# Reordering the stages of a phase on TensorE: convolution stages in one stretch, transposition and linear layer in another

## The chip, the cores and the metric

The kernel runs on one core of one Trainium2 chip. The metric is the time of one execution in microseconds on the device. The engines of the core are TensorE (PE; its weight loads are shown as PEld), VectorE (DVE), ScalarE (ACT), GpSimd (POOL) and SyncE (SP), which issues the DMAs. Each has its own queue and works through it in order; semaphores order the engines against one another.

## The reference

Input x holds 128 samples of 32 channels by 512 positions. Four layers follow one another. Each applies to x a chain of modulated one-dimensional convolutions (32 to 32 channels, 3 taps, weights scaled per sample by a style vector), and then a linear map over the 512 positions, with a residual:

```python
TYPES = ('same', 'upsample', 'same', 'downsample')
for i, typ in enumerate(TYPES):                       # convolutions of a layer
    out = _layer(out, style, weights[i], biases[i], mod_w[i], mod_b[i], typ)
# then, with y = out, a linear map of layer l over the last axis, added to x:
#   l = 0: y @ W.T + bias + low-rank updates (the same for all samples)
#   l = 1: y @ W_base.T + b + mixture of 8 low-rank adapters, top 2 by a router
#   l = 2: y @ kernel + bias + low-rank update per sample block (gate) + shared one
#   l = 3: y @ W_up.T + 4 low-rank experts, the best one by gate_w + expert_bias
```

All of it is in float32.

## The kernel before, in words

**Data.** 128 samples are 8 groups of 16. A group is a tile of 128 partitions (4 blocks of 32 channels) by 4 rows by 512 positions. A *phase* n is one layer of one group; groups go in pairs, so `PHASES` is 32, `STEP` is 8 phases for the four layers of a pair, `layer(n)` is `n % 8 // 2`. The residual stream of a group stays in SBUF in `x[g]`.

**Set-up.** A first program (about 68 us) makes the tables of scales and the effective weights. The main program follows.

**Convolution part of phase n** (small tiles, several at once on the array, fp32):
- `conv0(n)` (L1009, matmuls at L1003): first convolution, reads `xs` (x scaled, by POOL, L716). 96 matmul instructions, tiles of 32 by 32.
- `products(n)` (L1017, matmuls at L1027): products of the weights of two convolutions, from `w2s` (POOL, L685); ACT copies them out (`raw_v`, `wv`; L760, L762), POOL sums them to the blurred weights `wv` (`blurred`, L698, three instructions). 160 short matmuls.
- `conv2(n, 0)` and `conv2(n, 1)` (L1033, matmuls at L1052): upsampling, blur and third convolution in one, even and odd positions; 112 matmuls each. Evacuated to `y2` by ACT (L747) and DVE (L861), then DVE corrects the two ends (L868, semaphore `y2_ends`).
- `down(n, 0)` and `down(n, 1)` (L1058, matmuls at L1068): last convolution, 48 matmuls each, evacuated to `y3` (ACT L753, DVE L875).

**Linear part of phase m** (full array):
- `turn(m)` (L1073): 16 transpositions; ACT makes the high part `y3t_hi` (L768), DVE the low part `y3t_lo` (L881). The two parts are float32r, and a product is made of three passes (`PASSES`: hi by hi, hi by lo, lo by hi).
- `base(m, b)` (L1133, matmuls at L1137), four blocks b of 12 matmuls, then on DVE `residual(m, b)` (L895).
- In layers 1 and 3 `adapter` (L1081), `to_tokens` (L1111), a routing chain `gated` on DVE (L909), `adapter_turn` (L1123) and `adapted` (L1142).
- In two phases of eight (`EFF`: `m % 8` is 1 or 4, both in layers without adapters) `effective` (L1099): four matmuls, added by DVE to `w_raw` giving `w_sum` (L957), the weights of layer 2 of a later phase.

**Banks.** The eight PSUM banks are two sets of four, `bank_a` and `bank_b`, with fixed parts: `bank_b` takes `conv0`, `conv2(·,0)`, the adapters, `base` and `effective`; `bank_a` takes `products`, `conv2(·,1)`, `down` and `turn`.

**Order before.** PE's queue is written out by hand (L1178 to L1212). Iteration n, with m = n - 1: `conv0(n)`, `turn(m)`, `conv2(n,0)`, `conv2(n,1)`, the adapter and first block or blocks of the linear layer of m, `products(n+1)`, the rest of the linear layer, `down(n,0)`, `down(n,1)`. So the linear layer of the phase before lies inside the convolutions of this one. The loops of the other engines (POOL L706, ACT L808, DVE L969, SP L635) follow this order. `effective` goes in halves into the banks that blocks 0 and 1 have used, and PE waits for DVE's addition before block 2.

Of the kernel before, what the change touches and what calls it, by code (L numbers as in the profile page):

```python
# [9 lines left out]
P = 128  # L10
# [42 lines left out]
PAD = 2  # L53
# [431 lines left out]
def main_program(nc, ctx, io, keep, scratch):  # L485
# [38 lines left out]
    z_ps, logit_ps = bank_b[0], bank_b[1]  # L524
    zt_ps = logit_ps

    lin_ps = [bank_b[2], bank_b[3], bank_b[0], bank_b[1]]
# [75 lines left out]
    with nc.Block() as block:  # L603
# [74 lines left out]
        def _(pool):  # L678
# [26 lines left out]
            blurred(0)  # L705
            for n in range(PHASES):  # L706
# [11 lines left out]
                if n - 1 in MADE_IN:  # L718
                    u = MADE_IN[n - 1]
                    raw = w_sum if u % USES in (2, 3) else w_raw  # L720
                    for k in range(KB):
                        pool.wait_ge(w_hi, made(u, k + 1))
                        nc.gpsimd.tensor_tensor(w[u % 2][1][:, k], raw[:, k], w[u % 2][0][:, k].bitcast(F32),
                                                ALU.subtract).then_inc(w_lo, 1)
                if l < LAYERS - 1:
# [4 lines left out]
                if n + 1 < PHASES:  # L730
                    scaled_weights(n + 1)
                    blurred(n + 1)

        @block.scalar
        def _(act):
            a = nc.scalar

            def evacuate_0(n):
                act.wait_ge(c0_done, n + 1)
                for r in ON_ACT:  # L740
                    a.activation(y0[:, r, PAD:PAD + LEN], bank_b[r][:], ACT.Identity, bias=column(n, T_B, r), scale=column(n, T_A, r)).then_inc(y0_act, 1)  # L741

            def evacuate_2(n, u):
                scale, bank = (T_A + 2, T_A2)[u], (bank_b, bank_a)[u]
# [4 lines left out]
            def evacuate_3(n):  # L749
                for u in range(2):  # L750
                    act.wait_ge(dn_done, 2 * n + u + 1)
                    r = ON_ACT[u]
                    a.activation(y3[:, r], bank_a[r][:], ACT.Identity, bias=keep["cb3"][:, layer(n):layer(n) + 1], scale=column(n, T_A + 3, r)).then_inc(y3_act, 1)  # L753

            def products(n):
# [3 lines left out]
                for r in range(ROWS):  # L759
                    a.activation(raw_v[:, r, 1:RAW + 1].rearrange("p k o -> p (k o)"), bank_a[r][:, 0:RAW * CH],  # L760
                                 ACT.Copy).then_inc(raw_ready, 1)
                    a.activation(wv[:, r, TAPS_V:].rearrange("p k o -> p (k o)"),  # L762
                                 bank_a[r][:, RAW * CH:(RAW + GHOSTS) * CH], ACT.Copy).then_inc(ghosts_ready, 1)

            def turned(m):
                for k in range(KB):
                    act.wait_ge(tr_done, tiles(m, k + 1))
                    a.activation(y3t[0][:, k], bank_a[k][:], ACT.Copy).then_inc(y3t_hi, 1)  # L768

            def adapter(m):  # L770
# [3 lines left out]
                if l == 1:  # L774
                    a.activation(z_raw[:], z_ps[:], ACT.Copy)
                    a.activation(logits[:], logit_ps[0:E1], ACT.Copy).then_inc(z_raw_ready, 1)
                elif l == 3:
                    a.activation(z_raw[0:Z23], z_ps[0:Z23], ACT.Copy).then_inc(z_raw_ready, 1)
# [6 lines left out]
            def adapter_turned(m):  # L785
                if layer(m) in (1, 3):
                    rows = E1 * R1 if layer(m) == 1 else len(PASSES) * E3 * R3
                    act.wait_ge(zt_done, before(m, (1, 3)) + 1)
                    a.activation(zt[0][0:rows], zt_ps[0:rows], ACT.Copy).then_inc(zt_hi, 1)
# [18 lines left out]
            for n in range(PHASES + 1):  # L808
                m, convolve, linear = n - 1, n < PHASES, n > 0
                if convolve:  # L810
# [3 lines left out]
                if convolve:  # L814
                    evacuate_2(n, 0)
                    evacuate_2(n, 1)
                if linear:
                    adapter(m)
                    exponentials(m)
                if n + 1 < PHASES:  # L820
                    products(n + 1)
                if linear:
# [3 lines left out]
                if convolve:  # L826
                    evacuate_3(n)

        @block.vector
        def _(dve):  # L830
# [20 lines left out]
            def evacuate_0(n):  # L851
                dve.wait_ge(c0_done, n + 1)
                for r in ON_DVE:
                    v.tensor_scalar(y0[:, r, PAD:PAD + LEN], bank_b[r][:], column(n, T_A, r), column(n, T_B, r),  # L854
                                    ALU.mult, ALU.add).then_inc(y0_dve, 1)

            def evacuate_2(n, u):
                scale, bank = (T_A + 2, T_A2)[u], (bank_b, bank_a)[u]
# [12 lines left out]
            def evacuate_3(n):  # L871
                for u in range(2):
                    dve.wait_ge(dn_done, 2 * n + u + 1)
                    r = ON_DVE[u]
                    v.tensor_scalar(y3[:, r], bank_a[r][:], column(n, T_A + 3, r), keep["cb3"][:, layer(n):layer(n) + 1],  # L875
                                    ALU.mult, ALU.add).then_inc(y3_dve, 1)

            def turned(m):
                for k in range(KB):
                    dve.wait_ge(y3t_hi, tiles(m, k + 1))  # L880
                    v.tensor_tensor(y3t[1][:, k], bank_a[k][:], y3t[0][:, k].bitcast(F32),  # L881
                                    ALU.subtract).then_inc(y3t_ready, 1)

            def residual(m, b):
# [10 lines left out]
                v.tensor_tensor(result, lin_ps[b][:], x[g][:, b], ALU.add).then_inc(x_ready, 1)  # L895
# [13 lines left out]
            def gated(m):  # L909
# [6 lines left out]
                if l == 1:  # L916
                    then(v.tensor_copy(lg[:], logit_ps[:, 0:ROWS * E1].rearrange("p (t e) -> p t e", e=E1)))
                else:
                    then(v.tensor_tensor(lg[:, :, 0:e], z_ps[:].rearrange("p (t c) -> p t c", c=P)
# [413 lines left out]
```

## Time and profile before

| | us |
|---|---|
| median of 3 runs | 1300.11 |
| lowest, highest | 1298.98, 1308.33 |
| profiled execution, its time | 1306.01 |
| its span, first to last instruction | 1304.2 |
| mean granted clock of TensorE | 0.987 |

| engine | busy us | share of the span |
|---|---|---|
| PE (matmuls) | 1233.0 | 95% |
| PEld (weight loads) | 704.6 | 54% |
| POOL | 546.2 | 42% |
| DVE | 496.3 | 38% |
| ACT | 356.1 | 27% |

The span comes from one profiled execution; the runs without a profile give the median. A row of the timeline gives the start, the duration of the row (from the first start to the last end, where it holds several instructions), engine, line, operation, output and inputs, number of instructions, and in brackets the idle time ahead of it with what ended it. Ends of matmuls are modelled, so that the distance between two starts says more than a duration. The granted clock is that which the chip let TensorE have, 1.00 being 2.4 GHz and 0.50 being 1.2 GHz.

### The profile page before, as it was taken

How to read it: one execution, taken by the hardware profiler on the slowest of the kernel's cores; microseconds unless marked ns; L12 is line 12 of the kernel's file. 1: busy time of each engine (PE TensorE's matmuls, PEld its weight loads, DVE VectorE, ACT ScalarE, POOL GpSimd, SP SyncE). 2: the span in 40 equal slices, each digit the busy share in tenths (PEclk: the TensorE clock that was granted, in tenths of full speed). 3: DMA queues.
4: the chain of work that ended last, by engine and by line, in shares of the span. 5: the costliest groups of instructions: out<-in, count | busy, mean ns of one | idle time of the engine just before them, and what ended most of it. 6: DMA issues, size and time to landing. Idle time of an engine off the chain costs nothing.

```text
span 1304.2 us, 45847 instructions
## 1 busy us (share of the span) xinstructions
PE 1233.0 (95%) x21400; PEld 704.6 (54%) x21400; DVE 496.3 (38%) x975; ACT 356.1 (27%) x757; POOL 546.2 (42%) x417
## 2 busy tenths in 40 slices
PE   5847999999999999999999999999999999999997
PEld 5323556555555555565565555565565554665555
DVE  5612324344333333434333333434333434433343
ACT  2213313223322222313223222312323222312321
POOL 3156641444443442644323543644413544634400
PEclk9968999999999999999999999999999999999999
DMA  8232300002221200000301300000211200000101
GB/s 285 114 105 101 115 17 2 2 3 59 98 105 62 99 3 2 3 2 25 134 27 42 131 3 2 2 2 13 103 53 58 99 3 2 2 2 3 67 2 65
DMA packets 20828, 65.66 MB, mean 50 GB/s; under 512 B 4032, under 2 KB 4416, under 8 KB 16160
## 3 DMA queue, kind: packets, MB, share of 16 engines
q1 hardware_dynamic: 18960, 60.85, 12.8%
q8 instruction: 168, 2.75, 0.9%
q10 hardware_dynamic: 1680, 1.89, 0.5%
q14 instruction: 20, 0.16, 0.0%
HBM read 43.85 MB, written 18.87 MB: 48 GB/s over the span
## 4 chain that ended last, share of the span: by engine, by line
PE 87%; DVE 4%; POOL 1%; issue 1%; ACT 0%; DMA 0%; DVEq 0%; POOLq 0%
PE bank_b L1137 26%; PE bank_a L1068 13%; PE bank_a L1052 11%; PE bank_b L1052 11%; PE bank_b L1003 8%; PE bank_b L1095 5%; PE bank_a L1078 5%; PE bank_a L1027 3%; PE bank_b L1149 2%; PE bank_b L1118 1%; DVE w_sum L957 1%; PE bank_b L1130 1%; POOL xs L716 1%; POOL sum_v L698 1%; DVE z L939 1%
## 5 line engine op out<-in xcount | busy, mean ns | idle before, releaser
L698 POOL TENSOR_TENSOR sum_v<-raw_v 128x768 f32<-128x768 f32 x32 | 58.9, 1842 | 626.5 <-ACT raw_v L760 626.5
L1137 PE MATMUL bank_b<-w_hi,y3t_hi 128*128 128x512 f32 x512 | 210.0, 410 | 12.4 <-DVE w_sum L957 12.1
L1137 PE MATMUL bank_b<-w_hi,y3t_lo 128*128 128x512 f32 x512 | 203.0, 396 | 2.2 <-issue 2.2
L1137 PE MATMUL bank_b<-w_lo,y3t_hi 128*128 128x512 f32 x512 | 202.4, 395 | 0.1
L1068 PE MATMUL bank_a<-y,w_down 64*32 64x512 f32 x3072 | 173.6, 594 | 1.5 <-ACT wv L762 1.5
L1052 PE MATMUL bank_a<-y,wv 32*64 32x512 f32 (+2 forms) x3584 | 145.8, 480 | 2.3 <-issue 2.3
L1052 PE MATMUL bank_b<-y,wv 32*64 32x512 f32 (+2 forms) x3584 | 142.3, 480 | 1.8 <-ACT y L741 1.8
L895 DVE TENSOR_TENSOR x<-bank_b,x 128x512 f32<-128x512 f32 x96 | 66.4, 692 | 202.2 <-PE bank_b L1137 166.0
L753 ACT ACTIVATE y<-bank_a,cb,tab 128x512 f32<-128x512 f32 x64 | 49.7, 776 | 319.4 <-PE bank_a L1068 319.4
L1003 PE MATMUL bank_b<-xs,cw 32*32 32x512 f32 x3072 | 112.0, 615 | 15.3 <-POOL xs L716 15.3
L1137 PEld LDWEIGHTS bank_b<-w_hi,y3t_hi 128*128 128x128 f32 x512 | 96.8, 189 | 50.9 <-DVE w_sum L957 15.6
L1137 PEld LDWEIGHTS bank_b<-w_hi,y3t_lo 128*128 128x128 f32 x512 | 96.6, 189 | 25.9 <-issue 3.1
L1068 PEld LDWEIGHTS bank_a<-y,w_down 64*32 64x32 f32 x3072 | 55.3, 106 | 102.2 <-issue 102.2
L1137 PEld LDWEIGHTS bank_b<-w_lo,y3t_hi 128*128 128x128 f32 x512 | 97.0, 189 | 20.3 <-issue 0.6
L716 POOL TENSOR_TENSOR xs<-x,tab 128x512 f32<-128x512 f32 x96 | 97.3, 1043 | 8.9 <-DVE x L895 8.9
L1052 PEld LDWEIGHTS bank_a<-y,wv 32*32 32x32 f32 (+1 forms) x3584 | 45.0, 114 | 100.9 <-issue 100.4
L875 DVE TENSOR_SCALAR y<-bank_a,tab,cb 128x512 f32<-128x512 f32 x64 | 51.8, 810 | 121.4 <-PE bank_a L1068 121.4
L1003 PEld LDWEIGHTS bank_b<-xs,cw 32*32 32x32 f32 x3072 | 48.0, 104 | 76.5 <-issue 48.1
L854 DVE TENSOR_SCALAR y<-bank_b,tab 128x512 f32<-128x512 f32 x64 | 48.9, 807 | 100.8 <-PE bank_b L1003 100.8
L1052 PEld LDWEIGHTS bank_b<-y,wv 32*32 32x32 f32 (+1 forms) x3584 | 44.7, 114 | 76.4 <-issue 73.3
L881 DVE TENSOR_TENSOR y3t_lo<-bank_a,y3t_hi 128x512 fp32r<-128x512 f32 x128 | 79.5, 684 | 15.0 <-ACT y3t_hi L768 15.0
L861 DVE TENSOR_SCALAR y<-bank_a,tab 128x512 f32<-128x512 f32 x64 | 48.9, 806 | 90.4 <-PE bank_a L1052 90.4
(172 smaller groups left out, 1553.0 us busy)
## 6 DMA issues: line engine op xcount, KB each, us to landing
w_hi<-w_scratch SPq DMA_DIRECT2D x9, 1024.0 KB, 5.8
w_lo<-w_scratch SPq DMA_DIRECT2D x9, 1024.0 KB, 8.0
x_in<-in_x SPq DMA_DIRECT2D x32, 256.0 KB, 4.1
out_x<-out_tile SPq DMA_DIRECT2D x32, 256.0 KB, 2.4
w_raw<-w_scratch SPq DMA_DIRECT2D x3, 1024.0 KB, 9.8
w_scratch<-w_hi SPq DMA_DIRECT2D x3, 1024.0 KB, 3.9
w_scratch<-w_lo SPq DMA_DIRECT2D x3, 1024.0 KB, 6.9
w<-in_w SPq DMA_DIRECT2D x2, 1024.0 KB, 13.5
```

The lines of the kernel that those rows point to most:

```text
L698: ins = g_.tensor_tensor(dst[:, :, at:at + count].rearrange("p r k o -> p r (k o)"), src[:, :, 0:count].rearrange("p r k o -> p r (k o)"), ...
L716: nc.gpsimd.tensor_tensor(xs[:, b, 1:LEN + 1], src[:, b], column(n, T_S, b).broadcast_to((P, LEN)), ALU.mult).then_inc(xs_ready, 1)
L753: a.activation(y3[:, r], bank_a[r][:], ACT.Identity, bias=keep["cb3"][:, layer(n):layer(n) + 1], scale=column(n, T_A + 3, r)).then_inc(y3_ ...
L875: v.tensor_scalar(y3[:, r], bank_a[r][:], column(n, T_A + 3, r), keep["cb3"][:, layer(n):layer(n) + 1], ALU.mult, ALU.add).then_inc(y3_dve, 1)
L881: v.tensor_tensor(y3t[1][:, k], bank_a[k][:], y3t[0][:, k].bitcast(F32), ALU.subtract).then_inc(y3t_ready, 1)
L895: v.tensor_tensor(result, lin_ps[b][:], x[g][:, b], ALU.add).then_inc(x_ready, 1)
L1003: ins = pe.matmul(banks[r][CH * c:CH * (c + 1)], weights[rows, l, block_], src[rows, (r + c) % ROWS, 1 + shift:1 + shift + LEN], start=(i ...
L1052: ins = pe.matmul(banks[r][to:to + CH * count, at:at + length], wv[rows, a, tap:tap + count].rearrange("p t o -> p (t o)"), y0[rows, a, st ...
L1068: ins = pe.matmul(bank_a[2 * u + h][CH * a:CH * (a + 1)], keep["down"][rows, layer(n), t], y2[u][rows, c, t:t + LEN], start=(t == 0), stop ...
L1078: ins = pe.transpose(bank_a[k][:, P * b:P * (b + 1)], y3[:, b, P * k:P * (k + 1)], ident[:])
L1095: ins = pe.matmul(ps[0:rows], a_l[ai][:, k, col:col + rows], y3t[yi][:, k], start=(k == 0 and i == 0), stop=(k == KB - 1 and i == 2))
L1137: ins = pe.matmul(lin_ps[b][:], y3t[yi][:, k, P * b:P * (b + 1)], w[use(m) % 2][wi][:, k], start=(k == 0 and i == 0), stop=(k == KB - 1 an ...
```

## The change

The order of an iteration n (m = n - 1) becomes: `conv2(m,0)`, `conv2(m,1)`, `products(n)`, `down(m,0)`, `down(m,1)`, `conv0(n)`, then `turn(m)` and the whole linear layer of m. The bank sets take turns: in phase m `banks_p(m)` takes `conv2(m,0)`, `products(m+1)`, `conv0(m+1)` and then `base(m)`, and `banks_q(m)` takes `conv2(m,1)`, `down(m)`, `turn(m)`, the adapters and `effective(m)`. The first block of the linear layer is split into its high passes (which wait for each quarter of `y3t_hi`) and its low passes. `effective` is done in one piece behind block 0. On POOL `blurred(n)` moves from the end of iteration n - 1 into iteration n, behind `xs(n)` and the low parts of the weights, and ahead of the additions of the output bias (`xb_ready`); `scaled_weights(1)` goes ahead of the loop. ACT's and DVE's queues follow. What is computed stays the same, and so does the number of instructions of each kind; SP's part of the code is not touched.

```diff
-    z_ps, logit_ps = bank_b[0], bank_b[1]
-    zt_ps = logit_ps
-    lin_ps = [bank_b[2], bank_b[3], bank_b[0], bank_b[1]]
+    def banks_p(m):
+        return (bank_a, bank_b)[m % 2]
+    def banks_q(m):
+        return (bank_b, bank_a)[m % 2]
+    # z_bank, logit_bank, zt_bank: banks_q(m)[0], [1], [2]
...
             scaled_weights(0)
             blurred(0)
+            scaled_weights(1)
             for n in range(PHASES):
...
+                if n:
+                    blurred(n)
                 if l < LAYERS - 1:
...
-                if n + 1 < PHASES:
+                if 1 <= n and n + 1 < PHASES:
                     scaled_weights(n + 1)
-                    blurred(n + 1)
...
             def conv0(n):
-                if n >= 2:
-                    pe.wait_ge(x_ready, tiles(n - 2, ROWS))
-                    if (n - 2) % STEP in EFF:
-                        pe.wait_ge(w_sum_ready, summed(n - 2) + KB)
                 pe.wait_ge(xs_ready, tiles(n, ROWS))
+                pe.wait_ge(raw_ready, tiles(n, ROWS))
+                pe.wait_ge(ghosts_ready, tiles(n, ROWS))
...
             def products(n):
                 if n:
-                    pe.wait_ge(y2_ends, 2 * n)
+                    pe.wait_ge(y2_ends, 2 * n - 1)
...
             def conv2(n, u):          # u == 0
+                    if n:
+                        pe.wait_ge(y3t_ready, tiles(n - 1, KB))
+                        if (n - 1) % STEP in EFF:
+                            pe.wait_ge(w_sum_ready, summed(n - 1) + KB)
                 elif n:
-                    pe.wait_ge(y3t_ready, tiles(n - 1, KB))
-                banks = (bank_b, bank_a)[u]
+                    pe.wait_ge(x_ready, tiles(n - 1, ROWS))
+                banks = (banks_p(n), banks_q(n))[u]
...
             def down(n, u):
                 pe.wait_ge(y2_ends, 2 * n + 2)
-                if n + 1 < PHASES:
-                    pe.wait_ge(raw_ready, tiles(n + 1, ROWS))
-                    pe.wait_ge(ghosts_ready, tiles(n + 1, ROWS))
...
+            def base_hi(m, b):
+                for k in range(KB):
+                    if b == 0:
+                        pe.wait_ge(y3t_hi, tiles(m, k + 1))
+                    for wi in range(2):
+                        pe.matmul(banks_p(m)[b][:], y3t[0][:, k, P * b:P * (b + 1)], w[use(m) % 2][wi][:, k],
+                                  start=(k == 0 and wi == 0), stop=False)
+            def base_lo(m, b):        # the four lo passes; b == 0 waits for y3t_ready of each k
...
+            def weights(m):
+                if m + 1 < PHASES:
+                    pe.wait_ge(y0_act, evacuated(m + 1))
+                    pe.wait_ge(y0_dve, evacuated(m + 1))
...
+            def linear_plain(m):
+                weights(m)
+                base(m, 0)
+                effective(m)
+                for b in range(1, ROWS):
+                    base(m, b)
+            def linear_adapted(m):
+                weights(m)
+                base_hi(m, 0)
+                adapter(m)            # its hi passes first, then its lo passes
+                base_lo(m, 0)
+                to_tokens(m)
+                base(m, 1)
+                base(m, 2)
+                adapter_turn(m)
+                base(m, 3)
+                pe.wait_ge(zt_ready, before(m, (1, 3)) + 1)
+                for b in range(ROWS):
+                    adapted(m, b)
...
             for n in range(PHASES + 1):
                 m, convolve, linear = n - 1, n < PHASES, n > 0
+                if linear:
+                    conv2(m, 0)
+                    conv2(m, 1)
+                if linear and convolve:
+                    products(n)
+                if linear:
+                    down(m, 0)
+                    down(m, 1)
                 if convolve:
                     conv0(n)
                 if linear:
                     turn(m)
-                # ... conv2(n), adapter, blocks, products(n + 1), blocks, down(n)
+                    linear_adapted(m) if layer(m) in (1, 3) else linear_plain(m)
```

## Rows read from the trace of the kernel before

**Rows 1.** The page: PE's busy time, and the chain by engine.

```profile
PE 1233.0 (95%) x21400; PEld 704.6 (54%) x21400; DVE 496.3 (38%) x975; ACT 356.1 (27%) x757; POOL 546.2 (42%) x417
...
PE 87%; DVE 4%; POOL 1%; issue 1%; ACT 0%; DMA 0%; DVEq 0%; POOLq 0%
```

**Rows 2.** Timeline of PE: five starts of `down` (start us, us, then the instructions).

```profile
534.10 5.38 PE L1068 MATMUL bank_a<-y,w_down 64*32 64x512 f32 x96
...
577.38 5.38 PE L1068 MATMUL bank_a<-y,w_down 64*32 64x512 f32 x96
...
612.74 5.39 PE L1068 MATMUL bank_a<-y,w_down 64*32 64x512 f32 x96
...
645.39 5.38 PE L1068 MATMUL bank_a<-y,w_down 64*32 64x512 f32 x96
...
682.48 5.38 PE L1068 MATMUL bank_a<-y,w_down 64*32 64x512 f32 x96
```

**Rows 3.** Timeline of PE: the iteration from 612.74 to 645.39.

```profile
618.05 3.40 PE L1003 MATMUL bank_b<-xs,cw 32*32 32x512 f32 x96
621.39 1.97 PE L1078 MATMUL bank_a<-ident,y 128*128 128x128 f32 x16
623.29 4.45 PE L1052 MATMUL bank_b<-y,wv 32*64 32x512 f32 x112
627.67 4.45 PE L1052 MATMUL bank_a<-y,wv 32*64 32x512 f32 x112
632.04 0.50 PE L1137 MATMUL bank_b<-w_hi,y3t_hi 128*128 128x512 f32 x1
632.38 0.40 PE L1137 MATMUL bank_b<-w_lo,y3t_hi 128*128 128x512 f32 x1
...
634.71 0.40 PE L1137 MATMUL bank_b<-w_hi,y3t_lo 128*128 128x512 f32 x1
635.04 1.85 PE L1027 MATMUL bank_a<-w2s,w_up 32*32 32x96 f32 x160
636.82 0.51 PE L1137 MATMUL bank_b<-w_hi,y3t_hi 128*128 128x512 f32 x1
```

**Rows 4.** Timelines of ACT and DVE in the same iteration.

```profile
622.84 2.06 ACT L768 ACTIVATE y3t_hi<-bank_a 128x512 fp32r<-128x512 f32 x4
...
623.47 2.48 DVE L881 TENSOR_TENSOR y3t_lo<-bank_a,y3t_hi 128x512 fp32r<-128x512 f32 x4 [0.44 <-ACT y3t_hi L768]
...
632.25 1.53 DVE L861 TENSOR_SCALAR y<-bank_a,tab 128x512 f32<-128x512 f32 x2 [2.65 <-PE bank_a L1052]
633.81 0.17 DVE L868 TENSOR_TENSOR y<-y,tab 128x8 f32<-128x8 f32 x1
```

**Rows 5.** Waits (total us, times, longest); timeline of the copies in layer 1.

```profile
PE bank_b L1137 <- DVE w_sum L957: 12.1, 8, 1.5
...
559.07 0.40 PE L1137 MATMUL bank_b<-w_hi,y3t_hi 128*128 128x512 f32 x1
...
559.76 0.57 ACT L776 ACTIVATE logits<-bank_b 8x512 f32<-8x512 f32 x1
```

**Rows 6.** Timeline of PE: the start of the main program.

```profile
83.96 5.16 PE L1003 MATMUL bank_b<-xs,cw 32*32 32x512 f32 x96 [11.76 <-POOL xs L716]
...
101.74 2.48 PE L1027 MATMUL bank_a<-w2s,w_up 32*32 32x96 f32 x160 [2.03 <-DVE y L868]
105.76 6.76 PE L1068 MATMUL bank_a<-y,w_down 64*32 64x512 f32 x96 [1.54 <-ACT wv L762]
116.07 4.68 PE L1003 MATMUL bank_b<-xs,cw 32*32 32x512 f32 x96 [3.54 <-POOL xs L716]
...
146.84 5.38 PE L1068 MATMUL bank_a<-y,w_down 64*32 64x512 f32 x96
```

**Rows 7.** Timeline of PE inside `products`; then busy times, granted clock by window.

```profile
172.93 0.94 PE L1027 MATMUL bank_a<-w2s,w_up 32*32 32x96 f32 x67 [1.63 <-issue]
...
174.00:176.00 2.00, 2.00 (x5) 1.61 (x6) 0.00 (x0) 1.27 (x8) 0.77 (x1) 0.50 0.03 8
```

## What bounds the kernel, what the change does to it, and the forecast

> **What bounds the kernel now.** I read the page's first part and its chain, then the timeline of TensorE (PE) over whole iterations, then ScalarE (ACT) and VectorE (DVE) in the same stretch, then the waits and the start. PE is busy in 95% of the span and carries 87% of the chain [rows 1]; apart from its own weight loads no other engine passes 42%. So only three things can move the time: what PE issues (unchanged in kind and number by this edit), the gaps at the edges between stages, and the waits.
>
> An iteration runs from the start of one `down` stage to the next. Its length is 43.28 us where the linear layer is that of layer 1 (534.10 to 577.38), 35.36 us in layers 0 and 2 with the weight update `effective` (577.38 to 612.74), 32.65 us without it (612.74 to 645.39), and 37.09 us in layer 3 (645.39 to 682.48) [rows 2]. From the `down` that starts at 146.84 [rows 6] thirty iterations follow (linear phases m = 1 to 30: 7 plain, 8 with update, 8 of layer 1, 7 of layer 3). Besides these there is the start, up to 146.84, and the tail.
>
> **The change part by part, PE first.**
>
> *Edges.* A full-array matmul follows another after 0.23 us (632.38 stands behind a first one that took 0.34) [rows 3]. So a full-array stretch behind small tiles costs 0.11 us at its first matmul. A small stage behind a full-array one starts 0.33 us after the last matmul instead of 0.23 (634.71 to 635.04) [rows 3], 0.10 us. `products` alone has both edges, inside the linear layer; after the change it stands between `conv2` and `down`, and the full-array work is one stretch. `turn` to the linear layer loses its edges too. Per iteration about 0.3 us of edges goes. The Trainium skill, "TensorEngine Tiling (Array Packing)", section Key Properties, says that a change of tiling mode drains TensorE; the rows agree that it costs something. The sum goes by the rows, and its full worth is a rival below.
>
> *The wait before `down` (new).* `down(m)` needs both evacuations of `conv2(m,1)` and the end correction. Before, a block of the linear layer and `products` lay between. Now only `products(n)` does, 1.78 us (635.04 to 636.82) [rows 3]. In the rows `conv2(·,1)` ends at E = 632.04 (start of the next stage), DVE evacuates from 632.25 for 1.53 us and the correction starts at 633.81 for 0.17 us [rows 4], so it ends at E + 1.94. To PE's start I add 0.11, between 0.05 and 0.15 (in the start-up, where nothing covers this chain, PE stood 2.03 us on it [rows 6]). `down` starts at E + 2.05, whatever `products` gains by following without a change of tile shape. Shown as idle time this is 0.2 us if `products` runs as before, up to 0.8 if it starts during the end of `conv2`. Behind this wait stand `down`, `conv0`, `turn` and all the rest of PE's queue.
>
> *The wait before the linear layer (new).* Call C the start of `turn`, 621.39. ACT first evacuates `conv0`, then starts `y3t_hi` at 622.84 = C + 1.45; four take 2.06 us, so the ends lie at C + 2.05, 2.54, 3.02, 3.51. DVE's `y3t_lo` start at 623.47 and take 2.48 us for four: ends C + 2.8 to C + 4.56 [rows 4]. Before, 8.75 us of `conv2` hid all of it. Now the first block wants `hi` at C + 2.10: two matmuls per quarter, 0.23 each plus about 0.1 where the weight load is exposed; the eight end at C + 4.06. The four `lo` matmuls follow without a further wait; the block ends at C + 4.99. Before, `turn` and first block took 1.90 + 3.00 = 4.90 us. The split into hi and lo passes is what makes the new wait cheap: waiting for all of `lo` would give C + 4.61 + 2.79 = C + 7.4.
>
> *Plain iteration.* down 5.31, conv0 3.34, turn and block 0 4.99, three blocks of 12 matmuls 8.37, edge 0.09, two `conv2` 8.75, to the next `down` 2.05: 32.90 against 32.65, +0.25 us. The evacuations of `down`'s second half (under 1 us) hide under `conv0` (3.34); the raw copies on ACT (1.4 us) under `down`.
>
> *With update.* Before, PE waits for `w_sum` 12.1 us in 8 waits [rows 5], since the blocks share the banks of the update. The four products of the update (0.93) now go to the banks that `turn` has left, and DVE's additions have three blocks (8.4 us) before `conv2` wants the banks. 32.90 + 0.93 = 33.83 against 35.36: -1.53 us.
>
> *Layer 1.* ACT copies `z_raw` and then `logits`; the latter starts at 559.76 and takes 0.57, so it ends 1.26 us after PE's next matmul starts (559.07) [rows 5]. The cover was a whole block (2.79), now four matmuls (0.93): about +0.38. The gating chain on DVE had block 1 and `products`, now blocks 1 and 2 (5.6 us), and gives back 0.1. Together +0.5 us. *Layer 3*: one short copy, hidden; 37.51 against 37.09, +0.4 us.
>
> *Other queues.* POOL now runs `blurred(n)` (about 6.3 us) behind `xs(n)` and the low parts of the weights; it waits for the raw copies, some 12 us into the iteration, ends at about 18 and is wanted at over 32. `xb` (5 us) and `w2s` behind it end at about 24; `w2s` is wanted 8.75 us into the next iteration. SP waits for `xb` before its loads of x, and these are wanted an iteration later. In layer 3 the last two residuals wait for output tiles to be stored; they end about 3.9 us after PE leaves the linear layer, and `conv2(·,1)` wants them at 4.4: nothing, with little room.
>
> *Start.* Before, POOL makes `wv(1)` ahead of `xs(1)`, so that `conv0(1)` starts at 116.07 with a wait of 3.54, and `products(1)` stands 2.03 us for the evacuations; then `down` runs 6.76 instead of 5.38 us at the lower clock [rows 6]. After: `w2s(1)` goes ahead of `xs(0)` (+0.83), so `conv0(0)` starts at 84.8 (was 83.96 [rows 6]), `conv2` at 91.7 (behind its evacuation), which ends at 100.5, `down(0)` 102.55, `conv0(1)` 107.9, `turn(0)` 111.2, the linear layer ends at 124.6, two `conv2` to 133.4, `down(1)` at 135.5. `xs(1)` needs the x tile, which is reloaded after `xb(0)` (89.7): ready by about 99. That is 11.3 us ahead of 146.84. Not all of it is sure: two stalls of PE on nothing the profile names lie in that stretch before and may come again. I take 10 us; bounds 0 and 11.3.
>
> *Tail.* Layer 3's four last matmuls stand at the end, so the residuals start later; the wait for all of `lo` goes. I make this +0.5 us.
>
> **Sum.** 7 x 0.25 + 8 x 0.51 + 7 x 0.42 - 8 x 1.53 = -3.5 us over thirty iterations. 1304.2 - 10 - 3.5 + 0.5 = 1291.2 us of span; with the 1.8 us around it 1293.0 against the profiled 1306.01. The median of before is 1300.11, 0.45% less than that run: 1287 us.
>
> **The rivals.**
>
> *The clock falls (slower).* At 174 to 176 us the granted clock is 0.50 (1.2 of 2.4 GHz), behind a stall of 1.63 us inside `products`; in these 2 us PE ran five full-array matmuls, where 0.23 us apart gives nearly nine; over the 3 us that it lasted I put the loss at 1.4 us [rows 7]. `down` at that clock lost 1.38 us [rows 6]. Against it: eight waits of 1.5 us for `w_sum` [rows 5] fell at full clock. The place is `products` plus the wait before `down`, 2 to 2.6 us of thin work in each of 30 iterations; it decides if the idle time reaches about 1.5 us. Then 30 x 1.4 = 42 us: 1329. The Trainium skill, "TensorE: Matmul & The Clock Gate", sections HAM oscillation and Part 4, warns of idle gaps and says that transposes don't count as busy. The second place would be `turn` plus its wait, 2.1 us. Chance 0.09.
>
> *Fetch stalls (slower).* PE shows eight waits on "issue" alone, the longest 1.63 [rows 7], all before 490 us, two of them in `products`. With `conv2` (224 matmuls) and `products` (160) now back to back, PE's queue is drained faster. One of 1 us per iteration gives 1287 + 30 = 1317. Part of each would vanish in the wait before `down`. Chance 0.08.
>
> *The start gives nothing* (x reload, or the same stalls and clock): 1287 + 10 = 1297. Chance 0.15.
>
> *The waits are longer*: if each quarter of the first block exposes its weight load and the output tiles bind, +0.4 us x 30: 1299. Chance 0.10.
>
> *The drains pay in full* (the rule of the tiling page as mechanism): the wait at the linear layer vanishes in what the edges give, -0.3 us x 30: 1278. It can't help at `down`, where the chain of evacuations sets the start. Chance 0.08.
>
> **Numbers.** My forecast holds with 0.50, by itself 1280 to 1295. The range of all but the two slow rivals is 1272 to 1304. 1% is 13 us, about what a measurement of this kernel can tell from no change; the forecast lies on that edge. Faster by over 1%: somewhat over half of the forecast's 0.50 and the drains, 0.36; slower 0.17; between them 0.47.
>
> **What would show it.** The waits for `w_sum` by L1137 gone. A wait of `down` for the correction on DVE, about 30 times, 0.2 to 0.8 us. A wait of the first block for `y3t_hi`. From `down` to `down` 32.9, 33.8, 43.8 and 37.5 us. `down(1)` at about 136. It is wrong if the granted clock in the regular part is below 1.00, if "issue" waits come in each iteration, or if `conv2(·,1)` waits for residuals.

## The result and the profile after

| | before | after |
|---|---|---|
| median, us | 1303.06 (4 runs) | 1343.41 (4 runs) |
| lowest, highest, us | 1298.98, 1308.33 | 1336.84, 1349.27 |
| profiled execution: time, span, us | 1306.01, 1304.2 | 1349.27, 1347.5 |
| mean granted clock in it | 0.987 | 0.976 |

The ratio is 1.0306, interval 1.0241 to 1.0371: slower by 3%, where no change or a gain of 1% was forecast. The time lies 39 us above the upper end of the range.

The page of the kernel after, its first part (busy time, share, instructions), the chain by engine, and the queue that brings the instructions (packets, MB, share):

```profile
PE 1249.6 (93%) x21400; PEld 719.4 (53%) x21400; DVE 503.4 (37%) x975; ACT 358.4 (27%) x757; POOL 547.2 (41%) x417
...
PE 82%; ACT 5%; issue 3%; DVE 3%; POOL 1%; DMA 0%; DVEq 0%
...
q8 instruction: 168, 2.75, 0.8%
```

PE issues the same 21400 matmuls, but "issue" stands at 3% of the chain where it was 1% [rows 1], and PE itself is busy 16.6 us longer. The waits of PE after (engine, tile, line, what it waited for: us in total, times, longest); the set-up and the first phase have been left out except for `xs`:

```profile
PE bank_a L1032 <- issue: 13.6, 8, 4.1
PE bank_b L1010 <- POOL xs L728: 12.5, 1, 12.5
...
PE bank_b L1032 <- issue: 10.7, 7, 2.4
...
PE bank_b L1074 <- issue: 9.9, 3, 4.5
...
PE bank_a L1074 <- issue: 3.6, 3, 2.9
PE bank_a L1146 <- ACT y3t_hi L781: 3.5, 16, 0.2
PE bank_a L1074 <- DVE y L879: 3.4, 8, 1.9
PE bank_b L1146 <- ACT y3t_hi L781: 3.3, 15, 0.2
```

The waits for `w_sum` [rows 5] are gone, and the new waits for `y3t_hi` are 0.2 us each, as forecast. What is new beyond that is "issue" in `products` (L1032) and in the `down` behind it (L1074). Over all lines "issue" holds 38.4 us in 23 waits, twelve of them of 1.85 us or more; before it was 7.4 us in eight, none as long as that.

Timeline of PE after, one iteration near the end and the stages at the start of the next:

```profile
1237.95 0.64 PE L1032 MATMUL bank_b<-w2s,w_up 32*32 32x96 f32 x23
1238.74 1.57 PE L1032 MATMUL bank_b<-w2s,w_up 32*32 32x96 f32 x128 [0.15 <-issue]
1242.21 0.27 PE L1032 MATMUL bank_b<-w2s,w_up 32*32 32x32 f32 x9 [1.90 <-issue]
1242.41 7.08 PE L1074 MATMUL bank_a<-y,w_down 64*32 64x512 f32 x96
1249.41 3.40 PE L1010 MATMUL bank_b<-xs,cw 32*32 32x512 f32 x96
...
1274.90 1.87 PE L1032 MATMUL bank_a<-w2s,w_up 32*32 32x96 f32 x148
1278.86 0.28 PE L1032 MATMUL bank_a<-w2s,w_up 32*32 32x32 f32 x12 [2.09 <-issue]
1279.07 5.38 PE L1074 MATMUL bank_b<-y,w_down 64*32 64x512 f32 x96
```

In both iterations PE issues 151 and 148 of the 160 matmuls of `products`, stands for 1.90 and 2.09 us with nothing that it waits for, and then issues the last ones. In the first of them two things are lost: the stall, and 1.70 us because `down` then takes 7.08 instead of 5.38 us [rows 2]. Windows over that place (us, busy time of PE, PEld, DVE, ACT, POOL with instructions, granted clock, DMA share, GB/s):

```profile
1240.00:1242.00 2.00, 0.31 (x26) 0.21 (x24) 0.08 (x1) 0.00 (x0) 0.00 (x0) 1.00 0.00 0
1242.00:1244.00 2.00, 1.79 (x33) 0.75 (x40) 0.00 (x0) 1.36 (x8) 0.14 (x1) 0.77 0.03 8
1244.00:1246.00 2.00, 2.00 (x24) 0.53 (x16) 0.00 (x0) 0.00 (x0) 1.92 (x2) 0.50 0.00 0
1246.00:1248.00 2.00, 2.00 (x42) 0.73 (x34) 0.81 (x1) 0.78 (x1) 1.92 (x2) 0.88 0.00 0
```

The clock is 1.00 while PE stands and 0.50 (1.2 GHz) just after. The DMA share is 0.00 during the stall: nothing competes for the DMA engines then.

**Where the 56.3 us are.** The forecast span was 1291.2, the measured one 1347.5. Up to `down(1)`, forecast at 136.8 and begun at 142.31, 5.5 us; from there to the last `down`, 50.6 us; the tail 0.3. The 50.6 I take apart with the timeline. Waits on "issue" from 142 us on are 34.8 us against 6.4 before, which the forecast had carried over: 28.4. The stages of `down`, without waits inside, take 25.0 us more than 31 times 5.31, against 1.2 before (that 1.2 lies in the last one, in both): 23.8. Of these, eight stages that ran partly at the lower clock make 16.4 (five of them 1.70 each, as the one shown, three 2.3 to 2.9), and eleven at full clock that are 0.3 to 1.0 us longer make 7.4. Together 52.2, where 50.6 are to be explained; the difference is waits for DVE that vanish where PE comes late anyway. Every other stage has its length: `conv0` 3.34, `turn` with its wait 2.19, the two `conv2` 8.56 in the median.

### The profile page after: what moved, and what is told of

It is laid out like the page before. It is cut to its first block, busy times and chain, and to the rows that moved or that the text cites. A ratio compares the mean times of both kernels' runs of the same rounds, so it can differ in the third digit from the quotient of the medians.

```text
span 1347.5 us, 45826 instructions
## 1 busy us (share of the span) xinstructions
PE 1249.6 (93%) x21400; PEld 719.4 (53%) x21400; DVE 503.4 (37%) x975; ACT 358.4 (27%) x757; POOL 547.2 (41%) x417
## 3 DMA queue, kind: packets, MB, share of 16 engines
HBM read 43.85 MB, written 18.87 MB: 47 GB/s over the span
## 4 chain that ended last, share of the span: by engine, by line
PE 82%; ACT 5%; issue 3%; DVE 3%; POOL 1%; DMA 0%; DVEq 0%
PE bank_a L1061 11%; PE bank_b L1061 11%; PE bank_a L1146 9%; PE bank_b L1146 9%; PE bank_b L1074 7%; PE bank_a L1074 7%; PE bank_b L1010 4%; PE bank_b L1154 4%; PE bank_a L1154 4%; PE bank_a L1010 4%; ACT y L754 3%; DVE y L872 2%; PE bank_b L1099 2%; PE bank_a L1099 2%; PE bank_b L1032 1%
## 5 line engine op out<-in xcount | busy, mean ns | idle before, releaser
L1074 PE MATMUL bank_b<-y,w_down 64*32 64x512 f32 x1536 | 100.7, 646 | 11.6 <-issue 9.9
L1146 PE MATMUL bank_a<-w_hi,y3t_hi 128*128 128x512 f32 x256 | 103.7, 405 | 3.5 <-ACT y3t_hi L781 3.5
L1146 PE MATMUL bank_b<-w_hi,y3t_hi 128*128 128x512 f32 x256 | 103.8, 405 | 3.3 <-ACT y3t_hi L781 3.3
L1074 PE MATMUL bank_a<-y,w_down 64*32 64x512 f32 x1536 | 97.2, 630 | 7.1 <-issue 3.6
L1146 PE MATMUL bank_b<-w_lo,y3t_hi 128*128 128x512 f32 x256 | 101.1, 395 | 0.0
L1146 PE MATMUL bank_a<-w_lo,y3t_hi 128*128 128x512 f32 x256 | 101.1, 395 | 0.0
L743 POOL TENSOR_TENSOR x<-x,ob 128x512 f32<-128x512 f32 x64 | 80.0, 1289 | 0.0
L709 POOL TENSOR_TENSOR wv<-sum_v 128x1024 f32<-128x1024 f32 x32 | 75.9, 2371 | 2.5
L1154 PE MATMUL bank_b<-w_hi,y3t_lo 128*128 128x512 f32 x256 | 70.0, 395 | 0.0
L1154 PE MATMUL bank_a<-w_hi,y3t_lo 128*128 128x512 f32 x256 | 70.0, 395 | 0.0
```

Of the source, the lines that this page charges most:

```text
L709: ins = g_.tensor_tensor(dst[:, :, at:at + count].rearrange("p r k o -> p r (k o)"), src[:, :, 0:count].rearrange("p r k o -> p r (k o)"), ...
L743: nc.gpsimd.tensor_tensor(x[g][:, b], src[:, b], keep["ob"][:, l], ALU.add).then_inc(xb_ready, 1)
L1074: ins = pe.matmul(banks_q(n)[2 * u + h][CH * a:CH * (a + 1)], keep["down"][rows, layer(n), t], y2[u][rows, c, t:t + LEN], start=(t == 0), ...
L1146: pe.matmul(banks_p(m)[b][:], y3t[0][:, k, P * b:P * (b + 1)], w[use(m) % 2][wi][:, k], start=(k == 0 and wi == 0), stop=False)
L1154: ins = pe.matmul(banks_p(m)[b][:], y3t[1][:, k, P * b:P * (b + 1)], w[use(m) % 2][0][:, k], start=False, stop=(k == KB - 1 and l in (0, 2)))
```

## The experiments

Two theories stood at the start. One (theory F): instructions don't reach PE's queue fast enough for `products` when `conv2` runs right before it; the clock's falls and the longer `down` follow from these stalls. The other: the time is lost to the new order as such, in the edges between shapes (rival S) or in the idle time before `down` (rival I; 2.2 us of thin work in each iteration), whatever the queue has. Each ratio is to the kernel before, run again on the same chip. The four experiments without a ratio have one run each, so that a few us between two of them say nothing.

### Products issued twice, in the old order

```diff
 # kernel before, products(n)
-for s, at, first, count in (*((t, CH * t, 0, TAPS) for t in range(TAPS)), ...):
+for s, at, first, count in 2 * (*((t, CH * t, 0, TAPS) for t in range(TAPS)), ...):
```

> The kernel before, with the matmuls of products issued twice (the same values are written again). 160 more matmuls per phase in the middle of the linear layer, 1.78 us each phase. Theory F: 640 instructions in 3.6 us are more than the fetches give (256 per 3.3 us), so each phase waits another 2 to 4 us on issue: span 1304 + 57 + 64 to 128 = 1425 to 1490, waits on issue 64 to 128 us. Rivals S and I: the order of before is kept and nothing idles, so the span is 1304 + 57 = 1361 with under 15 us on issue.

Measured: 1481.27 us, span 1479.5, clock 0.949, against 1304.09 of before. Waits, timeline and the DMA view of one place (the last from 640 to 650 us in 40 slices of 0.25 us):

```profile
PE bank_a L1027 <- issue: 81.3, 45, 2.9
```

```profile
641.49 1.78 PE L1027 MATMUL bank_a<-w2s,w_up 32*32 32x96 f32 x152
645.31 1.96 PE L1027 MATMUL bank_a<-w2s,w_up 32*32 32x32 f32 x128 [2.03 <-issue]
649.33 0.68 PE L1027 MATMUL bank_a<-w2s,w_up 32*32 32x32 f32 x40 [2.06 <-issue]
```

```profile
GB/s 0 0 0 0 0 0 0 0 0 0 0 0 66 0 0 0 0 0 0 0 0 0 0 0 0 0 0 66 0 0 0 0 0 0 0 0 0 0 0 0
DMA packets 2, 0.03 MB, mean 3 GB/s; under 512 B 0, under 2 KB 0, under 8 KB 0
...
q8 instruction: 2, 0.03, 1.1%
...
q8 instruction: 208, 3.41, 0.9%
```

Between the two stalls PE issues 128 matmuls, with their weight loads 256 instructions. Two packets arrive in these 10 us, both in the queue of instructions; they start at about 643.1 and 646.9, and each stall ends 2.2 to 2.4 us after such a start. Over the whole run (last line) there are 208 packets where before has 168; 40 more for 5120 more matmuls and as many loads: one packet, 16 KB, for 256 instructions. In the records of all nine traces no two of them start closer than 3.25 us. `products` uses 320 instructions in 1.78 us [rows 3], so 256 of them in 1.4.

Besides the 57 us that the doubled matmuls take by themselves, 85.9 us of "issue" (all lines) came, where before has 7.4. The doubled part lies in the old place, between blocks of the linear layer, with no edge and no wait added. The stalls come from the burst itself: the theory of the queue holds, and one that needs the new place can't explain this run.

The Trainium skill, "Runtime: NRT & Kernel Launch", section Instruction fetch mechanics, says that instructions are brought in blocks of 16 KiB, 256 of them, and that this is mostly hidden because an engine dispatches more slowly than blocks arrive. The block size agrees with 256 instructions from stall to stall; that it is hidden doesn't, where PE uses a block in 1.4 us and none follows another in under 3.25.

### Shorter products, in the new order

```diff
 # kernel after, products(n), from phase 2 on: two of the five steps, 64 of 160 matmuls (phase 1: four steps)
-for s, at, first, count in (*((t, CH * t, 0, TAPS) for t in range(TAPS)), ...):
+for s, at, first, count in ((0, 0, 0, TAPS), (2, 2 * CH, 0, TAPS)):
```

> The changed kernel, with 64 instead of 160 matmuls in products from phase 2 on (the middle one of three taps and the edge terms are left out, so part of the computation is missing). Everything else stays, and down still starts when the evacuations of conv2 are done. Theory F: 192 instructions fewer per iteration behind conv2, so the waits on issue fall from 38 us to under 10, and the span to about 1305, although PE now idles 1.2 to 1.9 us before each down. Rival I: the idle time before down is longer than in the changed kernel, so the clock falls oftener and the span is at or above 1347.

Measured: 1289.18 us, span 1287.4, clock 0.990. Waits, and the timeline: a `down`, the `turn` behind it, and the four next starts of `turn` (layer 1, update, plain, layer 3 between them):

```profile
PE bank_a L1074 <- DVE y L879: 18.4, 16, 1.9
PE bank_b L1074 <- DVE y L879: 16.7, 16, 1.1
...
PE bank_b L1061 <- issue: 1.3, 1, 1.3
```

```profile
510.38 5.38 PE L1074 MATMUL bank_a<-y,w_down 64*32 64x512 f32 x96 [1.10 <-DVE y L879]
...
519.03 1.97 PE L1084 MATMUL bank_a<-ident,y 128*128 128x128 f32 x16
...
562.92 1.97 PE L1084 MATMUL bank_b<-ident,y 128*128 128x128 f32 x16
...
596.78 1.97 PE L1084 MATMUL bank_a<-ident,y 128*128 128x128 f32 x16
...
629.76 1.97 PE L1084 MATMUL bank_b<-ident,y 128*128 128x128 f32 x16
...
667.28 1.97 PE L1084 MATMUL bank_a<-ident,y 128*128 128x128 f32 x16
```

Less work in `products` can't shorten an iteration here, because `down` waits for the correction on DVE in its place: 1.10 us in 29 of 32 phases (35.1 in all), where the full `products` leave 0.2. So this run shows the new order with its waits and its edges as they are, and with a queue that is hardly ever short. "Issue" falls from 38.4 to 1.3 us. From 142 us on every `down` but one and the last takes 5.31 or 5.32 us, where after 19 of 31 take at least 0.28 us longer; the one takes 6.15, at full clock. The iterations are 43.89, 33.86, 32.98 and 37.52 us. That is the forecast of the prediction (43.8, 33.8, 32.9, 37.5), and the time with it; what I expected just before the run, about 1305, was 18 us too much. So the new order as such costs no more than the forecast had for it; the loss is the stalls and what follows on them.

The 29 idle stretches of 1.10 us before `down` brought no fall of the clock, so the thin work at that place isn't enough for one. The last `down`, which no `products` precedes, stands 1.92 us and then runs at the lower clock, 7.08 us.

### Products behind down

```diff
 # kernel after, order on PE; ACT's copies move along
     conv2(m, 1)
-    products(n)
     down(m, 0); down(m, 1)
+    products(n)
     conv0(n)
```

> The changed kernel with products between down and conv0. Nothing covers the evacuations before down, so PE idles about 2 us there in each of 31 iterations; products has left conv2. Theory F: waits on issue under 15 us; the idle time adds 1.8 us per iteration, about 55 us, to what the changed kernel would take without fetch waits (1291 to 1300): 1340 to 1355, a clock fall on a part of them. Rival I: 2 us of idle time lets the clock fall in most iterations, 1.7 us each: over 1390.

Measured: 1432.11 us, span 1430.3, clock 0.971: 77 us above the upper end expected, and in the range that rival I named (over 1390). The largest waits, and three stages of one iteration:

```profile
PE bank_b L1074 <- DVE y L879: 30.8, 16, 2.0
PE bank_a L1074 <- DVE y L879: 30.8, 16, 2.0
PE bank_a L1010 <- ACT wv L775: 24.7, 16, 1.6
PE bank_b L1010 <- ACT wv L775: 23.3, 15, 1.6
```

```profile
1147.94 7.08 PE L1074 MATMUL bank_a<-y,w_down 64*32 64x512 f32 x96 [1.92 <-DVE y L879]
1154.95 1.85 PE L1032 MATMUL bank_b<-w2s,w_up 32*32 32x96 f32 x160
1158.35 4.13 PE L1010 MATMUL bank_b<-xs,cw 32*32 32x512 f32 x96 [1.55 <-ACT wv L775]
```

Waits on "issue" fell to 7.9 us in six: behind `down`, which uses its 192 instructions in 5.31 us, `products` mostly finds the queue full. But `down` now stands 1.92 us in every iteration, and `conv0` 1.55 us more for ACT's copies of the products out of the banks that `conv0` writes. This second wait (48 us) I had overlooked: whatever is moved to the end of a stage takes its evacuation with it. So the run shows where the stalls go, and is no way to remove them. It also shows the other side of the clock: of the 31 `down` from 142 us on, each behind a wait of 1.92 to 1.98 us, ten ran at the lower clock at first and took 1.70 us longer, as the one shown (granted clock 0.56 from 1148 to 1151 us), with no "issue" wait ahead of them but one of 0.42 us. Idle time of this length lowers the clock sometimes, whatever PE waits for. Four `conv0` were slow in the same way (1.4 to 2.5 us longer, behind waits of 1.54 to 1.63 us, three of them with an "issue" wait inside the `products` ahead). Nine more `conv0` take 0.2 to 0.8 us longer at full clock, as the one shown (1.00 from 1158.4 to 1162.4 us): there the queue is short behind `products`, without a wait in the records. The falls are some 25 us in 14 iterations, not in most as rival I had it; without the 48 us of the second wait the span would lie under 1390.

### Conv0 between conv2 and down, products behind down

```diff
 # kernel after, order on PE; ACT, DVE and the waits follow
     conv2(m, 0); conv2(m, 1)
-    products(n)
+    conv0(n)
     down(m, 0); down(m, 1)
-    conv0(n)
+    products(n)
     turn(m)
```

> The changed kernel with another order of its small stages: conv2, conv2, conv0(n), down(m), products(n), turn(m), linear layer. The dense stage products no longer follows conv2; conv0 covers the evacuations that down waits for, and products covers those that turn waits for. Theory F (PE's instructions are fetched 256 at a time and never closer than 3.3 us apart, and products behind conv2 uses them faster): the waits of PE on issue fall from 38 us to under 10, the lower clock goes with them, and no wait of down for L879 is left; span 1278 to 1292. Rival S (small stages back to back cost by themselves, whatever their order): still over 1330. Rival I (the idle time before down lets the clock fall, and that is the loss): about as F here, so this run does not tell F and I apart.

Measured over three rounds: 1302.17 us (1299.69 to 1306.93) against 1304.09 (1300.49 to 1309.92), ratio 0.9987, interval 0.9969 to 1.0004. That is no difference, and 41 us less than the kernel after with the same instructions. Waits and one stall:

```profile
PE bank_a L1036 <- issue: 10.6, 7, 3.6
...
PE bank_b L1036 <- issue: 5.6, 6, 1.3
```

```profile
940.71 1.69 PE L1036 MATMUL bank_a<-w2s,w_up 32*32 32x96 f32 x140
...
943.73 0.31 PE L1036 MATMUL bank_a<-w2s,w_up 32*32 32x32 f32 x20 [1.34 <-issue]
```

The wait of `down` for DVE is gone, since `conv0` covers it. Stalls fell from 38.4 to 17.4 us (16 waits), not below 10 as expected. With the iterations of the run with shorter products and 0.3 us less in each of 30, the span would be 1278; the 16 us more of "issue" are most of what lies between that and 1300.2. The undisturbed iterations are 32.57, 33.5, 43.54 and 37.16 us, 0.3 shorter than those of the kernel after. So what runs ahead of `products` sets how often it stalls, but this burst can outrun the queue behind `down` too.

### Products in two parts, in the new order

```diff
 # kernel after, order on PE; ACT copies between its two evacuations of y3
     conv2(m, 1)
-    products(n)
+    products(n, 0)          # 64 matmuls
     down(m, 0)
+    products(n, 1)          # 96 matmuls
     down(m, 1)
```

> The changed kernel in its own order, nothing left out, with products cut in two: 64 matmuls behind conv2 as before, 96 between the halves of down. Theory F: the waits on issue fall from 38 us to under 10 and the clock stays up. The second part no longer hides in the wait for the evacuations, which costs 1.1 us and two changes of shape per iteration, 45 us in all against the run with short products (1287), so the span is 1320 to 1340. Rivals S and I (small stages back to back, or idle time before down, make the waits on issue): they stay near 38 us, and the span goes to 1365 or more.

Measured: 1339.29 us, span 1337.5, clock 0.985:

```profile
PE bank_a L1036 <- issue: 4.7, 3, 2.5
...
PE bank_b L1079 <- DVE y L881: 17.3, 16, 1.1
...
PE bank_a L1079 <- DVE y L881: 17.3, 16, 1.9
```

No matmul is left out and no edge taken away (two are added), and "issue" falls from 38.4 to 9.4 us: it is the burst's length that PE's queue can't follow. The time stays about where it was (at the upper end of what was expected), since the second part now lies in the open: `down(m, 0)` waits 1.10 us for DVE 28 times (34.6 in all), which the whole `products` had covered. Here, as in the run with shorter products, what fills the wait of `down` costs nothing, and what is taken out of it has to be paid elsewhere.

### Both: conv0 first, products in two parts

```diff
 # the kernel of "conv0 between conv2 and down", order on PE
     down(m, 0)
+    products(n, 0)          # 64 matmuls
     down(m, 1)
-    products(n)
+    products(n, 1)          # 96 matmuls
```

> The order of the spread kernel (conv2, conv2, conv0, down, products, turn), with products cut in two: its first 64 matmuls between the two halves of down, its last 96 behind down. No burst is longer than 192 instructions, under one fetch of 256. Theory F: waits on issue fall from 17 us to under 6; two more changes of tile shape cost 0.3 to 0.4 us per iteration (about 11 us), so the span is 1283 to 1296. If the waits on issue in the spread kernel have another cause than the burst, they stay at 15 us or more and the span is over 1305.

Measured over three rounds: 1299.84 us (1295.48 to 1304.05) against 1301.82 (1299.67 to 1308.51), ratio 0.9979, interval 0.9958 to 1.0000.

```profile
PE bank_a L1038 <- issue: 5.6, 5, 2.0
```

"Issue" is down to 8.6 us in eight waits, near the 7.4 of before, though not under 6 as expected. But the iterations are 32.88, 33.82, 43.85 and 37.48 us, again 0.3 longer than with `products` in one piece: two more edges between shapes, 0.15 us each. The gain in stalls (8.8 us) and the cost of the edges (30 times 0.3) cancel, and the two ratios, 0.9987 and 0.9979, can't be told apart. The span, 1296.1, lies just above the upper end expected.

### The update's banks alone, in the old order

The one term of the sum that gave a gain was that of the update. It doesn't need the new order: in the kernel before the matmuls of `effective` can also go to `bank_a`, which is free once the products have been copied.

```diff
 # kernel before, effective(m) on PE and DVE: all four products in one piece, behind block 1
-    for k in (2 * half, 2 * half + 1):
-        pe.matmul(bank_b[k][:], ...)
+    pe.wait_ge(raw_ready, tiles(m + 2, ROWS)); pe.wait_ge(ghosts_ready, tiles(m + 2, ROWS))
+    for k in range(KB):
+        pe.matmul(bank_a[k][:], ...)
 # linear layer
-    pe.wait_ge(w_sum_ready, summed(m) + 2)
 # down(n, 0)
+    pe.wait_ge(w_sum_ready, summed(n - 1) + KB)
```

> The kernel before with one part of the change alone: the four products of the update of the weights go, in one piece behind block 1, to the bank set that the linear layer doesn't use at that time (bank_a, free once the raw copies of products are out), so PE doesn't wait for w_sum. Order and banks of all else are those of before. Theory F: the 12.1 us of waits for w_sum are gone, the waits on issue stay at 7 to 10 us; span about 1292, ratio 0.990 to 0.993. If the gain of that part had been given back elsewhere (DVE late for the residuals, down waiting for w_sum), the span stays above 1300.

Measured over five rounds: 1292.79 us (1290.21 to 1298.93) against 1301.66 (1299.06 to 1309.78), ratio 0.9926, interval 0.9898 to 0.9953: faster by 0.7%, the best of all kernels here that compute everything. Its waits show none for `w_sum`, and "issue" at 7.6 us as before:

```profile
PE bank_b L1136 <- issue: 4.9, 5, 1.8
...
PE bank_a L1024 <- issue: 2.4, 2, 1.3
```

The waits for `w_sum` had been 12.1 us [rows 5], 0.9% of the time; 8.9 us came back.

## Why the prediction was wrong

**What held.** The lengths of the iterations: 32.9, 33.8, 43.8, 37.5 forecast, 32.98, 33.86, 43.89, 37.52 in the run with shorter products, and in the kernel after itself 37.50 where the queue isn't short (1279.07 to 1316.57). So the wait before `down` (0.21 us where it shows), the waits for `y3t_hi` (0.2), the end of the waits for `w_sum`, the price of layers 1 and 3 and the tail were right. That the plain iteration agrees within 0.1 us is in part luck, since three terms are off and cancel: two `conv2` take 8.57 us, not 8.75; from their end to `down` it is 2.18, not 2.05; `turn` and the linear layer take 13.59, not 13.45. The prediction took `products` behind `conv2` for no change of tile shape, but it is one, 32*64 to 32*32 [rows 3], and the full `products` take 1.97 us there instead of 1.78, which eats the cover of the wait. The start too: with no stall in it `down(1)` begins at 135.31 us in the run with shorter products, forecast 135.5 to 136 (the prediction counts two unnamed stalls up to 146.84 in the kernel before; the trace has one, 1.06 us at 137.60). The sum was right for a PE that always has its next instruction: 1291.2 us forecast, with the 7.4 us of "issue" of before in it, and 1287.4 measured there, with 1.3.

**The step that failed** is the one that costs the move of `products` at nothing but edges. I wrote that with `conv2` and `products` back to back "PE's queue is drained faster", priced it at one stall of 1 us per iteration (30 us) and gave it 0.08. It was the mechanism. Its size without what follows is 38.4 - 7.4 = 31 us, as that rival had it. That the size agrees is luck: there isn't one stall of 1 us per iteration but 23 in all, of 1.7 us on average. To this come 7.4 us in which `down` is starved at full clock without a wait in the records.

**The second rival came with it.** "The clock falls" was put down to the thin work of `products` and of the wait before `down` and given 0.09 as a case of its own. The shorter products, with 1.10 us of idle time at that place in 29 phases, show no fall there; the falls in the kernel after came where a stall of 1.85 us or more had gone before, in eight iterations, 16.4 us. So these weren't two rivals of which at most one comes: the second is what the first brings. Stalls, starved `down` stages and clock together, 31 + 7.4 + 16.4, are nearly all of the 56.3 us. With these three measured terms the forecast of the profiled run, 1293.0, becomes 1293 + 31 + 7 + 16 = 1347 us, against 1349.27. Of the signs that the prediction named for being wrong, two came: a granted clock below 1.00 in the regular part, and "issue" waits, though not in each iteration.

**What the rows had shown.** One could have seen it from the kernel before. Half of the reading was there: stalls on "issue" inside `products`, and a clock at 0.50 behind one of them [rows 7]. What was missing was a rate for each stage. 192 instructions of `down` take 5.31 us [rows 2], 192 of `conv0` 3.34, 448 of both `conv2` 8.75, 320 of `products` 1.78 [rows 3]; for 256 instructions that is 7.1, 4.5, 5.0 and 1.4 us, and in the linear layer, with one full-array matmul and its load every 0.23 us, about 30. Before, `products` stood between blocks of the linear layer, where the queue has all the time to fill; the change puts it behind 8.75 us of the stage that uses 256 in 5.0. The packets of instructions, 168 in the run, tell how many come at once.

**How a stall comes about.** All 23 stalls of the kernel after end 2.17 to 2.71 us after the start of a packet, and in 18 of them the packet before had started 4.2 us or more before that one (5.03 at the stall of 2.09 us). So it mostly isn't the least distance of 3.25 us that holds them up, but the time from asking for a packet to having it. Counting PE's records against the packets shows how far ahead the queue is filled (about 8 instructions per phase are not in the records, so the counts are good to some ten). In the slow linear layer a packet starts when some 250 to 300 instructions are still in hand, about one block. In the stalls of 1.85 to 2.16 us in or just behind `products` it starts 0.9 to 1.2 us after PE has begun its last block, with 45 to 91 instructions in hand, and these are used up in 0.4 to 0.65 us. From the start of the last block in hand to the end of the stall it is 3.4 to 3.7 us. So my estimate is that a block has to last some 3.5 us; in `conv2` it lasts 5.0, in `products` 1.4, and 3.5 less 1.4 is the size of these stalls. By this estimate, where in `conv2`, `products` or `down` a block happens to end decides whether an iteration has a stall, a longer `down` or neither.

**The longest stalls.** Those of 3.59, 2.91, 4.47 and 4.12 us (ending at 109.40, 147.15, 345.41 and 1042.36) are of another kind: their packet starts only 0.6 to 2.2 us after the stall has begun, at 107.20, 144.84, 343.18 and 1040.14, and just before that the kernel's own transfers are dense, 347 GB/s from 104 to 107 us, 342 from 142 to 144.8, 309 from 340 to 343 and 334 from 1036 to 1040 (columns as in the windows above):

```profile
1036.00:1040.00 4.00, 2.25 (x181) 1.78 (x149) 1.70 (x3) 1.45 (x2) 0.00 (x0) 1.00 0.85 334
```

In the 3 us ahead of the packets of the other stalls of 1 us and more it is 0 to 11 GB/s. That transfers delay the packets is likely by this, but no run moved them.

**What stays open.** Stalls in `products` come after 123 to 151 of its 160 matmuls; a kernel that moves one stage by a few instructions, to shift where the blocks end, wasn't run. Nor is it settled why a stall of 2.09 us at 1276.8 left the clock up and one of 1.90 at 1240.3 didn't; the rows only say that both happen.

## What to carry to other kernels

Count instructions per us, not only busy time, before packing short matmuls together: here a stage that used 256 instructions in 1.4 us went with 7.4 us of "issue" in the whole run between slow full-array matmuls, and with 38.4 us behind a stage that used 256 in 5.0 us. If a stall can be long enough to lower the clock, put both into one rival, with the slower stage behind it in its price. Where only one term of a reordering gives a gain, try that term alone: moving the update's four products to other banks gave 0.7%, and the whole new order lost 3%.

## What the runs showed of the hardware

- Packets of 256 PE instructions (16 KB) start at least 3.25 us apart in every trace here, even when the DMA engines carry nothing else. Between 1270 and 1290 us of the kernel after, with a stall of 2.09 us at 1276.8, the DMA view has four packets in all, in slices of 0.5 us:

```profile
GB/s 0 0 33 0 0 0 0 0 0 0 0 0 33 0 0 0 0 0 0 0 33 0 0 0 0 0 0 0 0 33 0 0 0 0 0 0 0 0 0 0
DMA packets 4, 0.07 MB, mean 3 GB/s; under 512 B 0, under 2 KB 0, under 8 KB 0
```

  The packet at about 1276.2 started 5.0 us after the one before it, and the stall ended 2.65 us after its start. Traffic of the kernel's own transfers is not what makes a stall of this length; it may be what makes those of 2.9 to 4.5 us longer, since their packets start late and behind 309 to 347 GB/s of it.
- A shortage shows in two ways: as a wait on "issue", and, where it is short, only as a stage that takes longer. At 305.78 us of the kernel after `down` has no wait inside and takes 0.29 us more than 5.31, at 181.78 it takes 1.00 more.
- Idle time of 1.10 us before a stage, 29 times with shorter products and 28 times with `products` in two parts, let the clock stay at 1.00. Longer idle time was followed by 0.50 in part of the cases: eight of eleven stalls of 1.85 us or more from 142 us on in the kernel after, ten of 31 waits of 1.92 to 1.98 us with `products` behind `down`. It isn't the length alone: 1.36 us were enough once (`products` in two parts, at 919.45), 1.63 in the kernel before [rows 7], and 2.09 weren't. In the kernel after, five `down` behind such stalls took 7.08 instead of 5.38 us, 1.7 us each, about as much as the stall ahead of it, and three lost 2.3 to 2.9.
- A change of shape between small tiles has a price as well, not only one between small tiles and the full array (0.11 and 0.10 us [rows 3]): two more of them lengthen the iteration by 0.31 us (32.57 to 32.88), about 0.15 each.
